# A decoder layer on one core: the first rounding pass of the feed-forward's inner rows moved from VectorE to ScalarE

## What is computed

```python
def _act_quant(x):
    scale = 127.0 / jnp.clip(jnp.max(jnp.abs(x), axis=-1, keepdims=True), 1e-05)
    xq = jnp.clip(jnp.round(x * scale), -128.0, 127.0) / scale
...
gate = jax.nn.silu(_bitlinear(x, w_gate))
up = _bitlinear(x, w_up)
return _bitlinear(gate * up, w_down)
```

## Time and profile before

| | us |
|---|---|
| median of 3 runs (3730.02 to 3734.52) | 3733.89 |
| the profiled execution, device time | 3732.63 |
| its span, first to last instruction | 3730.9 |
| busy, TensorE | 3615.0 (97%) |
| busy, VectorE | 3460.5 (93%) |
| busy, ScalarE | 3064.7 (82%) |
| busy, GpSimd | 2253.7 (60%) |

### The profile page before, as it was taken

How to read it: one execution, slowest core, us unless ns; L and a number is a source line. 1 busy time by engine, 2 the same in 40 slices (tenths; PEclk the granted TensorE clock), 3 DMA queues, 4 the chain that set the end, 5 groups by cost and what they waited for, 6 DMA issues and landing times. The chain is left out here.

```text
span 3730.9 us, 167466 instructions
## 1 busy us (share of the span) xinstructions
PE 3615.0 (97%) x71481; PEld 2282.1 (61%) x71481; DVE 3460.5 (93%) x9241; ACT 3064.7 (82%) x6357; POOL 2253.7 (60%) x2395
## 2 busy tenths in 40 slices
PE   6999999999999999999999987999999999999997
PEld 3666666665666666666666654666666666666664
DVE  8999999999999999999999987889988898888886
ACT  4999999999999999999999984677776677777675
POOL 3777777777777777777777764444444444444442
PEclk9999999999999999999999998999999999999998
DMA  2000221000000000000000000000000000100000
GB/s 82 25 25 25 56 59 53 25 25 25 25 25 25 25 25 25 25 25 25 25 25 25 25 26 18 24 24 24 24 24 24 24 24 28 32 24 24 24 16 10
DMA packets 99973, 104.27 MB, mean 28 GB/s; under 512 B 17297, under 2 KB 95005, under 8 KB 98729
## 3 DMA queue, kind: packets, MB, share of 16 engines
q1 hardware_dynamic: 99224, 93.56, 8.7%
HBM read 48.52 MB, written 17.53 MB: 18 GB/s over the span
## 5 line engine op out<-in xcount | busy, mean ns | idle before, releaser
L565 POOL TENSOR_TENSOR conv_products<-normed_features,conv_taps_by_token 128x256 f32<-128x256 f32 (+1 forms) x837 | 757.9, 919 | 530.2 <-ACT normed_features L348 530.1
L771 POOL TENSOR_TENSOR exps_of_both_halves<-scores 128x256 f32<-128x256 f32 x512 | 424.2, 851 | 583.8 <-ACT scores L1027 578.4
L295 PE MATMUL banks<-up_centred,after_cell_features 128*32 128x336 f32 x8928 | 740.3, 449 | 1.1 <-ACT after_cell_features L348 0.5
L295 PEld LDWEIGHTS banks<-up_centred,after_cell_features 128*32 128x32 f32 x8928 | 260.5, 109 | 277.6 <-issue 224.1
L302 PE MATMUL banks<-down,hidden_features 112*32 112x256 f32 x6696 | 419.2, 383 | 0.0
L578 POOL TENSOR_TENSOR conv_partial_sums<-conv_products,conv_partial_sums 128x512 f32<-128x512 f32 x279 | 370.5, 1328 | 21.9
L1027 ACT ACTIVATE scores<-scores 128x512 f32<-128x512 f32 x512 | 305.4, 626 | 77.7 <-DVE scores L1175 74.0
L366 ACT ACT_TABLE_LOAD x279 | 358.0, 1283 | 5.2
L381 ACT ACT_TABLE_LOAD x279 | 358.0, 1283 | 5.1
L1175 DVE SCALAR_TENSOR_TENSOR scores<-banks,score_top 128x512 f32<-128x512 f32 x512 | 327.9, 681 | 26.1 <-PE banks L857 25.5
L269 PE MATMUL banks<-recurrent_weights,h_features 64*32 64x256 f32 x8928 | 313.1, 379 | 0.3 <-DVE h_features L509 0.2
(11 more groups left out here) (222 smaller groups left out, 9933.3 us busy)
## 6 DMA issues: line engine op xcount, KB each, us to landing
layer_inputs<-layer_outputs SPq DMA_DIRECT2D x279, 96.0 KB, 2.0
layer_inputs<-in_x SPq DMA_DIRECT2D x280, 32.0 KB, 1.8
x_scratch<-layer_outputs SPq DMA_DIRECT2D x279, 32.0 KB
x_tokens<-in_x SPq DMA_DIRECT2D x32, 256.0 KB, 3.0
context_features<-in_ctx SPq DMA_DIRECT2D x32, 256.0 KB, 3.7
layers_out<-x_scratch SPq DMA_DIRECT2D x32, 256.0 KB, 2.8
out<-result SPq DMA_DIRECT2D x64, 128.0 KB, 1.8
up_centred<-in_ff_up SPq DMA_DIRECT2D x1, 2688.0 KB
```

Of the source, the lines that this page charges most:

```text
L295: mm = nc.tensor.matmul(bank[group(l), b, 0:UP], xmt[:, n, group(l)], up[:, l, n, at:at + UP], start=n == 0, stop=n == HALF - 1, skip_grou ...
L565: return nc.gpsimd.tensor_tensor(prod[:, i:i + n], xnt[:, j % NRING].rearrange("p n t -> p (n t)")[:, None, :].broadcast_to([P, n, HALF * ...
L771: nc.gpsimd.tensor_tensor(psum[:, i % RING, :], pr[:, i % RING, 0:S], pr[:, i % RING, S:2 * S], ALU.add).then_inc(halves_added, 1)
```

## The change

The first pass becomes an activation of ScalarE, `Identity` with a per-partition scale (`q127`) and a per-partition bias (`round_at`, a tile that holds the constant), 128x1024 fp32 in and out. For tile q (0 and 1) it stands in quad q of ScalarE's list after the quad's first two exponentials and ahead of the denominators. The second pass stays on VectorE: tile 0 in slot 1 behind `attended`, tile 1 in slot 4 behind the clips of heads 12 and 13 and ahead of `x1_centre`. It waits for the activation by a new semaphore, `h_rounded`. After the loop, for the last sequence, both activations come first on ScalarE, and VectorE does the two second passes.

```diff
-    QUANT, QUANT_H, X1_OPS, MOMENTS = 9, 12, 6, 8
+    QUANT, QUANT_H, X1_OPS, MOMENTS = 9, 10, 6, 8
...
+            def h_round_up(j, tt):
+                act.wait_ge(hquant_step, QUANT_H * j + ROUNDS + 3)
+                nc.scalar.activation(gate[:, tt, :], hf[:, tt, :], ACT.Identity, scale=q127[:, tt:tt + 1], bias=round_at[:]).then_inc(h_rounded, 1)
...
+                            if q < QT and j > 0:
+                                h_round_up(f, q)
                             denominators(j, q)
...
-            def h_round_up(j, tt):
-                round_up(tt, hf, gate, hquant_step, QUANT_H * j + ROUNDS + 3)
-
             def h_round_down(j, tt):
-                round_down(tt, gate, hq, hquant_step, h_quantised(j, tt))
+                dve.wait_ge(h_rounded, QT * j + tt + 1)
+                nc.vector.tensor_scalar(hq[:, tt, :], gate[:, tt, :], -ROUND, 127.0, ALU.add, ALU.min).then_inc(hquant_step, 1)
...
                     h_steps(f)
-                    h_round_up(f, 0)
...
-                        if s_ == 0:
+                        if s_ == 1:
                             h_round_down(f, 0)
-                        if s_ == 1:
-                            h_round_up(f, 1)
-                        if s_ == 2:
+                        if s_ == 4:
                             h_round_down(f, 1)
```

More of the change, by code:

```diff
@@ L623, in attend_and_feed @@
     eps = sb("eps2", [P, 1])
+    round_at = sb("round_at", [P, 1])
     x4t = sb("layers_out", [P, SLOTS, QT, D])
@@ L676, in attend_and_feed @@
     gu_ready, gate_done, h_done, hquant_step = sem("gu_ready"), sem("gate_done"), sem("h_done"), sem("hquant_step")
+    h_rounded = sem("h_rounded")
     hqt_ready, hqt_done = sem("hqt_ready"), sem("hqt_done")
@@ L711, in h_quantised @@
     def h_quantised(j, tt):
-        return QUANT_H * j + QUANT_H - 2 * (QT - 1 - tt)
+        return QUANT_H * j + QUANT_H - (QT - 1 - tt)
     with nc.Block() as block:
@@ L1164, in _ @@
             nc.scalar.preload_act_table_set(LOG_EXP)
+            h_round_up(f, 0)
+            h_round_up(f, 1)
             h_features(f)
@@ L1326, in _ @@
             nc.vector.memset(eps[:], EPS).then_inc(const_step, 1)
-            dve.wait_ge(const_step, 2)
+            nc.vector.memset(round_at[:], ROUND).then_inc(const_step, 1)
+            dve.wait_ge(const_step, 3)
             dve.sem_inc(consts, 2)
```

## The result

The changed kernel takes 3762.33 us (median of 4 runs, 3762.03 to 3763.07), the kernel before 3733.50 (4 runs, 3730.02 to 3734.52). The ratio is 1.0079, with a 95% interval of 1.0063 to 1.0095: slower by 0.8%. Ratios and intervals are taken over all runs of both kernels, so they can differ by up to 0.0003 from the quotient of two medians. The profiled execution took 3763.07, its span is 3761.3.

What follows compares the result with a forecast made beforehand. TensorE was taken as the bound, busy 44.26 of 44.80 us a turn. The forecast added 29 x 1.15 = 33.4, 2 x 0.05 and about 0.3 to 3732.63, giving 3766.4 us, range 3742 to 3775.

Steps and rivals of the forecast that it cites:

- Part 1: New ScalarE activation: 1.23 us each; the first fills idle time in quad 0, leaving the logarithm 0.05 late.
- Part 2: Slot 1 of VectorE: GpSimd's addition blocks the round down to 1.19 us, giving `scores(5)` a new wait of 0.44.
- Part 3: Quad 1 of ScalarE: second activation isn't covered, denominators delay `attended`, and head 12's clip comes 0.26 us late.
- Part 4: Slot 4 of VectorE: round down and `x1_centre` alternate with GpSimd's additions, making head 14's clip 1.63 us late.
- Part 5: Chain from head 14's clip to `out_project` pair 6: slack 0.48 us, so a turn loses 1.15.
- d: Lateness of head 14's clip in slot 4 against the kernel before, forecast at 1.63 us.
- The last turns and the end: Turns j = 30 and 31 lose 2 x 0.05 us; the final passes after the loop about 0.3.
- B's first form: VectorE gets in first in slot 1: d = 1.14, 0.66 us a turn, 3752 us; B's chance overall 0.27.
- second form: B with nothing blocked in slot 4: d = 0.86, 0.37 us a turn, 3744 us; B's chance overall 0.27.
- D, the relief: VectorE's lighter load removes the `scores(7)` wait and adds none: 29 x 0.23 = 6.7 us less, 3726; chance 0.06.
- The sum by engine time alone: Price difference of ScalarE's activation against VectorE's pass, 64 x 0.49 = 31 us; not used, as the first is mostly covered.

Runs made afterwards that it cites:

- e4: Changed kernel with one wait added on GpSimd: head 6's addition waits until the first round down is done; 3747.54 us, ratio 1.0038.
- e3: Changed kernel with both round downs moved ahead of `attended`, in slots 1 and 3; 3728.40 us, ratio 0.9987.
- e6: e3 with the first activation ahead of exponentials 4 and 5 and the first round down in slot 0; 3724.85 us, ratio 0.9979.
- e7: Kernel before, nothing on ScalarE, second round down moved from slot 2 to slot 3 ahead of `attended`; 3726.42 us, ratio 0.9982.
- e8: Kernel before, complete on VectorE, with the two activations added on ScalarE, writing a tile nothing reads; 3733.98 us, ratio 1.0000.
- e1: Changed kernel with the second round down moved from slot 4 to slot 3, ahead of `attended`; 3738.39 us, ratio 1.0015.

## Why the prediction was right

**Part 1 held.** The activation was put at 1.23 from three other shapes and is 1.23. The first is covered and the logarithm behind it is 0.05 late. VectorE saw nothing of that: `attended` is 0.01 late, since a logarithm that has not waited is recorded at 0.36, not 0.38.

**Part 2 held.** The addition was expected at 3053.15 and the round down at 3053.25 for 1.19; they came at 3053.12 and 3053.20 for 1.19 (3069.99 and 3070.07, less 16.87). The new wait of `scores(5)` was put at 0.44. Its record says 0.37, and the product starts at 3055.05, 0.45 after its old place. e4 shows the cause by changing only the order.

**Part 3 was too large.** Head 12's clip was put 0.26 late and is 0.15. The step that failed is the distance from the logarithm to `attended`, 0.92 from a place where the logarithm had waited for TensorE. Behind the second activation it was 0.85 (3074.16 to 3075.01). That, and the 0.05 of part 1 that never arrived at `attended`, are 29 x 0.1 = 3 of the 4 us between forecast and result.

**Part 4 held.** From head 12's clip to head 14's the alternation was worked out as 3.83 (3063.56 - 3059.73). It is 3.83 (3080.32 - 3076.49), with the round down at 0.98 and the two of `x1_centre` at 1.82. Both instructions of `x1_centre` and the pass in front of them take turns with GpSimd's additions, whose pair is 2.05.

**Part 5 held.** d - 0.48, with d measured, gives 1.04, and the turn is 1.05 longer. The waits are where they were expected, at exponential 15 and at `attended_lo`, with a third at GpSimd's additions for `denominators` of quad 3.

**The last turns and the end** were put at 0.4 together. Measured from one first K product to the next, turn j = 30 is 0.02 longer (44.99 against 44.97), and from the last turn's to the end of the span it is 0.46 longer (77.04 against 76.58): 0.48.

**The rivals.** B's first form, VectorE first in slot 1, was made real as e4: 0.55 a turn against 0.66 worked out. Its second form, with nothing blocked in slot 4, is not seen in any of the four runs with the pass there (x1_centre is 1.82 or 1.83 in all). Its price wasn't that of nothing blocked either: the 1.27 in it is today's distance, in which `x1_centre` is blocked once. D, the relief, came true in e3 and e6, by about the size that was given to it (0.2% and less), but only after second passes were put elsewhere. That size was partly luck: the prediction's 0.23 a turn stands in no row, where the wait at `scores(7)` is 0.20; e7 and e6 are 0.23 and 0.24 shorter. The rule behind D (the Trainium skill, Perfetto Trace Analysis, Optimizing Scalar/DVE Operations: if DVE is saturated, moving work to Scalar may pay) is not what made it: e7 has the same gain with nothing moved to ScalarE. VectorE was 90% busy, but it was bound at two places in the turn and idle in front of others.

The sum by engine time alone, 31 us, which the prediction set aside, comes nearer to the measured 29 us than the forecast's 34. That is a coincidence: e8 adds the same work to ScalarE and loses nothing, and e1 keeps both activations and loses 6 us.

## What to carry to other kernels

A busy engine is not by itself a reason to take work off it: here e7, which moves nothing to ScalarE, is as fast as e6, which moves both passes. What is left of a moved step needs a place too, and the best ones here were directly ahead of an instruction that waits for somebody else (e1, e6, e7). Before moving an instruction later in a list, find the next instruction behind it that another engine waits for, and measure that one's slack: here 0.48 us, and everything beyond it was lost at the full rate. Where GpSimd and VectorE hold each other up, ask who starts first at the new place; removing work elsewhere shifts that too, as in slot 1 here.

## What the runs showed of the hardware

- A blocked instruction isn't slowed, it is put behind the other: the same round down took 1.19 where GpSimd's addition had started 0.08 us ahead of it (the changed kernel), and 0.68 where the addition came behind it (e4). This is the rule of the Trainium skill (SBUF — State Buffer, Who interferes with whom: the first to issue holds the port for the whole instruction). The rows add a size: a blocked pass ends 0.55 behind GpSimd's instruction though it is 0.68 long by itself, so by this estimate some 0.13 of it overlap. In e6 it ends 0.55 behind as well.
- The longest blocked pass was 1.67 (e6): it stood behind the 1.16 us subtraction of the context's split.
- An `Identity` activation with scale and bias by partition, 128x1024 in fp32, is 1.23 us, with 1.14 until the next one starts.
